# Routed experts of the second layer with the weights as the loaded operand, two blocks of rows streamed against them

## What is computed

```python
top_w, top_i = lax.top_k(softmax(xf @ gate_w.T), 6)
h = silu(einsum('ecd,edi->eci', xb, w1)) * einsum('ecd,edi->eci', xb, w3)
ob = einsum('eci,eid->ecd', h, w2)
y = zeros((T, D)).at[t_s].add(ob[buf_idx] * w_s[:, None])
```

## Time and profile before

| | |
|---|---|
| median of three runs | 1563.26 us (1562.28 to 1563.59) |
| span of the profiled execution, first to last instruction | 1559.5 us |
| what the runs lie above that span | 2.8 to 4.1 us |
| mean granted TensorE clock over the span | 0.953 |
| moved by DMA | 269.12 MB, 173 GB/s on average |

### The profile page before, as it was taken

One profiled execution on the slowest core, in us unless ns is written; L12 is line 12 of the kernel. 1 busy time (PEld: TensorE's weight loads), 2 busy tenths in 40 slices (PEclk: granted clock), 3 DMA queues, 4 the chain that ended last, 5 costly groups with the idle time before them and its releaser, 6 DMA issues.

```text
span 1559.5 us, 23674 instructions
## 1 busy us (share of the span) xinstructions
PE 1332.1 (85%) x8228; PEld 808.5 (52%) x8228; DVE 997.9 (64%) x1752; ACT 738.5 (47%) x1259; POOL 595.8 (38%) x462
## 2 busy tenths in 40 slices
PE   0047565599999599899899999999999999999997
PEld 0023252244444365566565666666666666666664
DVE  8999988979897658888545444444444444444222
ACT  4466654645554453441255454444544444454332
POOL 2343443444342343320143444344444444444343
PEclk9987866799999799999999999999999999999999
DMA  3557545678996775541278898988989998898665
GB/s 104 170 163 199 148 115 136 130 195 178 230 239 161 192 224 168 169 132 40 95 188 209 199 210 200 206 201 201 208 192 219 194 205 207 202 208 170 116 105 75
DMA packets 224178, 269.12 MB, mean 173 GB/s; under 512 B 148608, under 2 KB 148736, under 8 KB 223936
## 3 DMA queue, kind: packets, MB, share of 16 engines
q1 hardware_dynamic: 187408, 175.58, 42.5%
q0 software_dynamic: 36656, 92.03, 29.6%
HBM read 167.87 MB, written 70.32 MB: 153 GB/s over the span
## 4 chain that ended last, share of the span: by engine, by line
PE 67%; DVE 21%; issue 5%; ACT 3%; DMA 2%; POOL 0%; SPq 0%; POOLq 0%; DVEq 0%; ACTq 0%
PE psG L1832 38%; PE psO L1881 20%; DVE wkFD L1371 5%; PE psH L1849 3%; DVE wkFD L1353 2%; DMA ST<-W 2%; PE psX L1793 2%; DVE wkFN L1346 2%; DVE wkFD L1342 2%; DVE Wlo L1632 2%; DVE wkFN L1378 1%; DVE wkFN L1356 1%; DVE wkFD L1363 1%; PE psX L1731 1%; DVE H L1651 1%
## 5 line engine op out<-in xcount | busy, mean ns | idle before, releaser
L1832 PE MATMUL psG<-Whi,XSp 128*128 128x352 f16 (+2 forms) x3000 | 671.4, 329 | 11.4 <-issue 9.8
L1832 PEld LDWEIGHTS psG<-Whi,XSp 128*128 128x128 f16 x3000 | 295.3, 100 | 211.7 <-issue 37.5
L1881 PE MATMUL psO<-Whi,HS 128*128 128x512 f16 (+1 forms) x1180 | 390.5, 383 | 0.5 <-DVE OB L1671 0.5
L1832 PE MATMUL psG<-Wlo,XSp 128*128 128x352 f16 (+2 forms) x1500 | 389.0, 329 | 0.0
L1072 POOL DMA_INDIRECT out<-OB,posb x128 | 202.7, 1584 | 416.4 <-ACT OB L1279 412.7
L1632 DVE SCALAR_TENSOR_TENSOR Wlo<-ST,Whi 128x1088 f16<-128x1088 f32 (+1 forms) x116 | 149.6, 1291 | 212.0 <-ACT Whi L1225 204.1
L1651 DVE SCALAR_TENSOR_TENSOR H<-H,psG 128x352 f32<-128x352 f32 (+1 forms) x215 | 105.3, 490 | 242.5 <-ACT H L1244 226.8
L1881 PE MATMUL psO<-Wlo,HS 128*128 128x512 f16 (+1 forms) x590 | 226.3, 384 | 0.0
L1244 ACT ACTIVATE H<-psG 128x352 f32<-128x352 f32 (+1 forms) x215 | 95.3, 443 | 235.0 <-PE psG L1832 226.9
L1832 PEld LDWEIGHTS psG<-Wlo,XSp 128*128 128x128 f16 x1500 | 149.2, 99 | 93.4 <-issue 7.8
L1881 PEld LDWEIGHTS psO<-Whi,HS 128*128 128x128 f16 x1180 | 117.2, 99 | 118.2 <-issue 5.4
(11 more groups left out here) (219 smaller groups left out, 1550.3 us busy)
## 6 DMA issues: line engine op xcount, KB each, us to landing
ST<-W SPq DMA_DIRECT2D x130, 544.0 KB
ST<-W SPq DMA_DIRECT2D x23, 512.0 KB
slots<-OB SPq DMA_DIRECT2D x39, 256.0 KB
wkK<-fT SPq DMA_DIRECT2D x32, 256.0 KB
xrows<-XG SPq DMA_DIRECT2D x20, 256.0 KB, 3.4
y0rows<-x SPq DMA_DIRECT2D x8, 512.0 KB, 5.3
y0rows<-OB POOLq DMA_DIRECT2D x16, 256.0 KB, 4.7
out<-OB SPq DMA_DIRECT2D x16, 256.0 KB
```

Of the source, the lines that this page charges most:

```text
L1832: op = M.matmul(o, hx[:, x, q * P:q * P + P], w(half_, off + c, nn), start=first, stop=last)
L1881: op = M.matmul(psO[bank(o)][:, :], hs(n)[:, x, q * P:q * P + P], columns[n](half_, off0 + q * 512, 512), start=(q == 0 and x == 0 and hal ...
```

## The change

In the routed part of the second layer two blocks make a pair, 64 pairs in all. Gate and up load a 128-column piece of the weights and stream 2 x 128 rows of x against it, from two neighbouring slots of `XSp`, which now lie in one buffer. The result has the inner columns on the partitions, as `down` wants them, so H is not turned. A pair has three tiles t = 3p + c: the first 128 gate columns with the first 128 of up, the second 128 of both, and the last 96 of gate with the last 32 of up, then 64 columns of up. For these 64 the high and the low part stand side by side as one loaded piece of 128 columns; streamed are x high and x low, so that all four products are made in 8 matmuls and the two halves of the partitions are added afterwards. The tiles use five PSUM banks in turn. ACT takes a tanh of each tile, DVE the products, ACT the high part and DVE the low part of H. The packed weights of the 32 experts are laid out anew (each piece has 1024 columns and 64 of the last 256; in SBUF with the low parts 1152), the one-hot buffers move into the gaps, x has four gather buffers instead of three, and the loop's order is written anew. Numbers and sizes of DMAs stay as they are. The core of the diff:

```diff
+def ring(z):
+    return z % 4 if z < 71 else (z - 71) % 4
+def ring_before(z):
+    return max(y for y in range(z) if ring(y) == ring(z))
+def place1(e):
+    return e % SLOTS1 * 4608 if e < 32 else 18432 + (e - 32) * 4352
+def spread(u):
+    return u // 1024 * 1152 + u % 1024
...
     for m, e in enumerate([32, 33] + list(range(32))):
         for c in range(4):
             pool = 2 <= m < SLOTS1
-            out.append((1, e, c * 1088, 1088, (m + 4) % SLOTS1 * 4352 + c * 1088, "pool" if pool else "dve"))
+            out.append((1, e, c * 1088, 1088, place1(e) + c * (1152 if e < 32 else 1088), "pool" if pool else "dve"))
     return out
...
-    yield "weight", R1
-    for j in range(NB1 + 2):
-        n = R1 + j
-        yield from ahead(n)
-        if n < NBLK:
-            yield "gu_pe", n
-            yield "gu", n
-        if 0 <= j - 1 < NB1:
-            yield "h_turn", n - 1
-        if 0 <= j - 2 < NB1:
+    def turn(n, pe):
+        if n < NBLK and by_pe(xslot(n)) == pe:
+            yield ("turn" if pe else "x_turn"), xslot(n)
+    def pair_weights(p):
+        if p >= 2:
+            ready = 63 + 4 * ((2 * p - 6) // 4) if p >= 3 else 59
+            yield from weights(2 if p < 6 else 1, min(ready, len(PIECES)))
+    def tile_in(t, what):
+        if 0 <= t < 3 * PAIRS:
+            yield what, t
+    yield "gather", R1 + 3
+    for n in (R1, R1 + 1):
+        yield from turn(n, True)
+        yield "weight", n
+    yield "clear", 0
+    for p in range(PAIRS + 1):
+        n = R1 + 2 * p
+        for m in (n + 4, n + 5):
+            if m < NBLK:
+                yield "gather", m
+        yield from turn(n + 2, False)
+        yield from tile_in(3 * p, "f_gu")
+        yield from tile_in(3 * p - 1, "f_split")
+        yield from pair_weights(p)
+        yield from tile_in(3 * p + 1, "f_gu")
+        if p < PAIRS:
+            yield "f_split", 3 * p
+        yield from turn(n + 2, True)
+        yield from tile_in(3 * p + 2, "f_gu")
+        yield from turn(n + 3, True)
+        if p < PAIRS:
+            yield "f_split", 3 * p + 1
+        if p >= 1:
             yield "down", n - 2
-        if j >= 3:
-            ready = 63 + 4 * ((j - 5) // 4) if j >= 5 else 59
-            yield from weights(2 if j < 12 else 1, min(ready, len(PIECES)))
+        yield from pair_weights(p)
+        if p >= 1:
+            yield "down", n - 1
+        for m in (n + 2, n + 3):
+            if m < NBLK:
+                yield "weight", m
     yield "end", 0
...
         A0 = RT[0][:, :, :].rearrange("p q c -> p (q c)").bitcast(F16).rearrange("p (n c) -> p n c", n=32)
         B0 = RT[1][:, 0:2, :].rearrange("p q c -> p (q c)").bitcast(F16)[:, 0:32 * NB0].rearrange("p (n j) -> p n j", n=32)
-        AB = [[W[:, at:at + 512].rearrange("p (r n) -> p r n", r=4) for W, at in pair]
-              for pair in (((Whi, 26112), (Whi, 26624)), ((Wlo, 26112), (Wlo, 26624)), ((Whi, 27136), (Wlo, 27136)))]
+        gaps = [Wlo[:, e * 4608:e * 4608 + 4608].rearrange("p (r n) -> p r n", r=4)[:, :, 1024:1152] for e in range(4)]
+        AB = [gaps[0:2], gaps[2:4], [W[:, 27136:27648].rearrange("p (r n) -> p r n", r=4) for W in (Whi, Wlo)]]
         idt = OT[:, 0:128]
+        XG1 = [XG[i][:, :] for i in range(3)] + [OH[:, 0:D + 32]]
+        FH = [RT[0][:, :, :].rearrange("p q c -> p (q c)")[:, i * 768:i * 768 + 768].rearrange("p (t c) -> p t c", t=3)
+              for i in range(2)]
+        FU = [RT[0][:, 3, i * 256:i * 256 + 256] for i in range(2)]
+        FS = [RT[1][:, :, :].rearrange("p q c -> p (q c)").bitcast(F16)[:, i * 1536:i * 1536 + 1536].rearrange(
+            "p (x t c) -> p x t c", x=2, t=3) for i in range(2)]
         idx = [sb("idx0", [P, 39], U32), posb[:, :].bitcast(U32)]
...
                 eng.wait_ge(b_gu, S1 + 2 * (z - S1) + 2)
             else:
-                eng.wait_ge(b_gu, R1 + z - 71 + 1)
+                eng.wait_ge(b_fgu, 3 * ((z - 71) // 2) + 3)
         def rows_stored(f):
...
+        def f_psum(t):
+            return (psG[0][0], psG[0][1], psG[1][0], psG[1][1], psH)[t % 5]
         l_bank = [psG[1][1], psX]
...
+                        x_there(eng, 70)
+                        x_read(eng, xslot(S1 - 3 + j))
+                    if j >= 4:
+                        x_read(eng, xslot(n - 4))
+                        eng.wait_ge(b_wsl, j - 3)
+                    to, there = XG1[j % 4], d_g1[j % 4]
                 G.indirect_dma_start(
-                    out=XG[g % 3][:, 0:w], out_offset=None, in_=X[l][:, :],
-                    in_offset=bass.IndirectOffsetOnAxis(ap=idx[l][:, j:j + 1], axis=0)).then_inc(d_g[g % 3], 16)
+                    out=to, out_offset=None, in_=X[l][:, :],
+                    in_offset=bass.IndirectOffsetOnAxis(ap=idx[l][:, j:j + 1], axis=0)).then_inc(there, 16)
             def down(n):
                 what, l, j = kind(n)
...
                     A.copy(hs(n)[:, 0, 0:w], bank_[:, 0:w]).then_inc(b_hshi, 1)
+            def f_gu(t):
+                p, c = divmod(t, 3)
+                rows = 96 if c == 2 else P
+                eng.wait_ge(b_fgu, t + 1)
+                if t == 0:
+                    eng.wait_ge(b_clear, 1)
+                if p >= 2:
+                    eng.wait_ge(b_flo, t - 5)
+                if c == 2:
+                    if p >= 2:
+                        eng.wait_ge(b_fh, t - 5)
+                    A.copy(FU[p % 2][0:64, :], f_psum(t)[64:128, 256:512]).then_inc(b_flow, 1)
+                A.activation(FH[p % 2][0:rows, c, :], f_psum(t)[0:rows, 0:256], ACT.Tanh,
+                             scale=0.5 * UN).then_inc(b_ftanh, 1)
+            def f_split(t):
+                p, c = divmod(t, 3)
+                eng.wait_ge(b_fh, t + 1)
+                if p >= 2:
+                    eng.wait_ge(b_down, R1 + 2 * p - 2)
+                A.copy(FS[p % 2][:, 0, c, :], FH[p % 2][:, c, :]).then_inc(b_fhi, 1)
             def h_low(n):
...
             def weight(n):
                 j = n - R1
-                g, e = NB0 + j, j // 4
-                eng.wait_ge(d_g[g % 3], 16 * (g // 3 + 1))
+                e = j // 4
+                gathered(eng, 71 + j)
                 if j >= 8:
-                    eng.wait_ge(b_outa, g - 7)
-                V.tensor_copy(WSL[:, n % 8:n % 8 + 1], XG[g % 3][:, D + e:D + e + 1]).then_inc(b_wsl, 1)
+                    eng.wait_ge(b_outa, NB0 + j - 7)
+                V.tensor_copy(WSL[:, n % 8:n % 8 + 1], XG1[j % 4][:, D + e:D + e + 1]).then_inc(b_wsl, 1)
+            def clear(_):
+                for i in range(2):
+                    op = V.memset(FH[i][:, 2, :], 0.0)
+                op.then_inc(b_clear, 1)
+            def f_gu(t):
+                p, c = divmod(t, 3)
+                rows = 96 if c == 2 else P
+                H, ps, gain = FH[p % 2][:, c, :], f_psum(t), 0.5 * XS * UN * UN
+                eng.wait_ge(b_ftanh, t + 1)
+                V.scalar_tensor_tensor(out=H[0:rows, :], in0=H[0:rows, :], scalar=1.0, in1=ps[0:rows, 0:256],
+                                       op0=ALU.add, op1=ALU.mult).then_inc(b_fsil, 1)
+                if c < 2:
+                    eng.wait_ge(b_fsil, t + 1)
+                    V.scalar_tensor_tensor(out=H, in0=H, scalar=gain, in1=ps[:, 256:512], op0=ALU.mult,
+                                           op1=ALU.mult).then_inc(b_fh, 1)
+                    return
+                U = FU[p % 2][0:64, :]
+                eng.wait_ge(b_flow, p + 1)
+                after(V.tensor_tensor(U, U, ps[0:64, 256:512], ALU.add))
+                eng.wait_ge(b_fsil, t + 1)
+                V.scalar_tensor_tensor(out=H[64:96, :], in0=H[64:96, :], scalar=gain, in1=ps[96:128, 0:256],
+                                       op0=ALU.mult, op1=ALU.mult)
+                V.scalar_tensor_tensor(out=H[0:64, :], in0=H[0:64, :], scalar=gain, in1=U, op0=ALU.mult,
+                                       op1=ALU.mult).then_inc(b_fh, 1)
+            def f_split(t):
+                p, c = divmod(t, 3)
+                eng.wait_ge(b_fhi, t + 1)
+                V.tensor_tensor(FS[p % 2][:, 1, c, :], FH[p % 2][:, c, :], FS[p % 2][:, 0, c, :],
+                                ALU.subtract).then_inc(b_flo, 1)
             def gu(n):
                 l, a = kind(n)[1], n % 2
...
+            def f_gu(t):
+                p, c = divmod(t, 3)
+                n = R1 + 2 * p
+                ps, s, at = f_psum(t), ring(xslot(n)), place1(p // 2)
+                if c == 0:
+                    for h in range(2):
+                        x_there(eng, xslot(n + h))
+                    for k in last_pieces(n):
+                        eng.wait_ge(*low(k))
+                if t == 0:
+                    eng.wait_ge(b_h, R1)
+                if t == 4:
+                    eng.wait_ge(b_hslo, R1)
+                if t >= 5:
+                    eng.wait_ge(b_fh, t - 4)
+                def x(which, q):
+                    return XSall[:, s:s + 2, which, q * P:q * P + P]
+                def sums(cols):
```

(76 more changed lines are left out.)

77 lines of the change are left out of this document (35 added, 42 removed).

## The result

The changed kernel takes 1626.53 us (median of 4 runs, 1617.93 to 1633.98) against 1563.42 us before: 1.0397 times as long, 95% interval 1.0351 to 1.0443. The forecast was 1546.6 us and faster, in a range of 1539 to 1560. The measured time lies 80 us above the forecast, on the other side of the kernel before.

A forecast was written before the change was run, and what follows sets the result against it. The prediction took PE, full in the last loop, as the bound. Span 1559.5 - 23.7 (PE work saved) + 7.0 (stalls at the ends) = 1542.8 us, with 3.8 from span to measured time 1546.6 us; range 1539 to 1560.

The forecast's parts named there:

- the order in a pair: Last loop: copies, splits, loads, transposes, gathers and scatters all arrive before PE needs them; costed at nothing.
- rival 3: ACT's in-order queue: late first pieces of 24 later experts hold tanh and copy of x, 0.35 us each; 1555 us, chance 0.09.
- The matmul of 256 columns: Gate and up on PE: 109.2 ns start to start, 68 a pair, 0.27 us more per pair than before.
- rival 2: Gate and up: two streamed pieces each pay a start, 112.6 ns a matmul; 1561.4 us, no difference; chance 0.07.
- rival 5: Gate and up: weight loads show, 151 ns a matmul, 1729 us; chance 0.03.
- The pair of 11.78 us: PE's work per pair in the last loop, 0.37 us less than before; 23.7 us saved over 64 pairs.
- the stall before pair 1: Loop start: no down ahead of pair 1, so PE waits for ACT's copy, tanh and copy of x; +1.75 us.
- the last split: Loop end: ACT's split of the last tile stands behind evictions of two downs, so down starts 1.9 us late.
- Rival 4: Last loop: DMA engines, at share 0.94, are the bound; a pair stays at 12.15 us, total 1570 us; chance 0.08.
- the sum for pieces 51 to 66: Pairs 2 to 5, four weight pieces each: stalls of 3.6, 2.9 and 0.2 us in pairs 3, 4, 5; 6.7 us.
- rival 1: First pairs flow: stalls from early pieces and the last split shrink to the old loop's; 1539 to 1541 us, chance 0.15.
- Rival 6: Pair loop runs half serial, a previous pair's buffer not free, each tile waiting for DVE; chance 0.01 where costing more than gained.

The follow-up runs named there:

- experiment 2: Changed kernel with a pair's two gathers and two weight-column copies ahead of the two downs, so before the scatters: 1547.35 us.
- experiment 1: Changed kernel with the first load of a new expert's four pieces ahead of the DMA transpose of x: 1582.9 us.
- experiment 5: Changed kernel with the two gathers between the two downs, behind the first scatter and ahead of the second: 1629.05 us.
- Experiment 8: Changed kernel with weight pieces spread two a pair from pair 1 on, gathers still behind the scatters: 1558.07 us.
- experiment 7: As experiment 5, but the next even block's DMA transpose is yielded in the pair before, ahead of the second weight piece: 1549.9 us.
- Experiment 3: Changed kernel with PE turning every block of the last loop, so no DMA transposes there: 1574.16 us.
- experiment 9: Changed kernel with gathers ahead of the scatters and weight pieces spread two a pair from pair 1 on: 1536.49 us.
- experiment 6: Control: changed kernel with only DVE's two routing-weight copies moved ahead of the downs, gathers still behind the scatters: 1634.24 us.

## Why the prediction was wrong

**What failed** is the paragraph on the order in a pair, which ended in "All this I cost at nothing". It cost 79 us, the difference between the changed kernel and experiment 2. Three things in it fell.

- *"its load stands behind the DMA transpose, which is free from tile 2 of the pair before on, 4 us before this pair."* I took the buffer's release as the transpose's only condition. It also waits for its gather, which stands on POOL behind two scatters, which wait for two evictions at the pair's end. The place of a moved step in each queue had to be followed through POOL as well as SP.
- *"Pieces land in 3.8 to 6.2 us, scatters in 4.9; ... only a landing of over 10 us would reach PE."* The rows were from the kernel before, where one scatter and one gather go out every 6 us (at 1202.12 and 1204.00, then at 1207.97 and 1209.86). With two gathers, two scatters, a transpose and a load within a few microseconds, gathers landed in 8.5 us (median), a piece behind a transpose in 9.7, and in experiments 1 and 5 a transpose behind a load in 11.8 to 13.4.
- *The margins were each taken from PE's own timetable.* Each of them held for one pair, and the steps close a ring. A ring has one length, the sum of all its links, and this one was 29.8 us where two pairs have 23.5. That ACT's queue then holds up everything behind a piece is rival 3. It was the right mechanism with a wrong size: 0.35 us for each of 24 experts, 8.4 in all. Experiment 8, where ACT no longer waits, gives 68 us back, some of them in the first pairs. But experiment 5 loses 82 us against experiment 2 without such waits, so rival 3 is one of two rings and not the whole.

**What held.** The matmul of 256 columns: 109.2 ns forecast and found (24 in 2.62 us), so rivals 2 and 5 fall. The Trainium skill's 81 ns for a load and a matmul of 128 columns ("TensorE: Matmul & The Clock Gate", Back-to-back issue gap) is not seen here either: the turn's eight matmuls of 128 columns, a load with each, take 0.45 us, 56 ns each. The prediction gave 120 ns at 256 columns as what follows from that figure, without a working, and it does not follow. The same section has 131 ns at 512 columns, and a straight line between the two gives 98 ns, an estimate below the 109 found. So the page did not speak for a slower kernel, and its 131 ns are not seen either: 18 matmuls of 512 columns take 3.88 us, 216 ns each. The pair of 11.78 us, found at 11.75 in experiment 2. ACT at 7.2 and DVE at 7.7 of 11.8 us a pair: in experiment 2 they are busy for 330 and 345 of 600 us, which is 6.5 and 6.8. The first tile, forecast for 768.5 and found at 768.04, and the stall before pair 1, forecast as 1.75 us and found as 1.36 (the changed kernel's timeline of PE):

```profile
768.04 0.38 PE L1988 MATMUL psG<-XSp,Whi 128*128 128x256 f16 x2 [1.15 <-ACT XSp L1300]
...
777.88 0.38 PE L1988 MATMUL psG<-XSp,Whi 128*128 128x256 f16 x2 [1.36 <-ACT XSp L1300]
```

The copy of x waited for in pairs 3 and 4, forecast as 3.6 and 2.9 us, found as 3.15 and 3.01:

```profile
813.46 0.61 PE L1917 MATMUL psX<-ident,XG 128*128 128x128 f16 x8 [3.15 <-ACT XSp L1300]
...
830.51 0.61 PE L1917 MATMUL psX<-ident,OH 128*128 128x128 f16 x8 [3.01 <-ACT XSp L1300]
```

And the last split, forecast at 1.9 us, found as 1.53:

```profile
1619.77 0.39 PE L2059 MATMUL psO<-Whi,RT 128*128 128x512 f16 x1 [1.53 <-DVE RT L1766]
```

Rival 4, full DMA engines, is refuted by experiments 2 and 7: the same transfers in another order, at 199 and 198 GB/s, and PE full. (Experiment 3 has fewer transfers and can't decide it.) The total forecast, 1546.6 us, is what the change gives once the ring is cut (1547.35). That does not save the prediction: it was made for the order in the diff. That the two numbers differ by less than 1 us is in part luck: experiment 2's stalls in the first pairs are some 2 us above their term, and 64 pairs of 11.75 us are 2 us below theirs.

**On the sum for pieces 51 to 66**: 6.7 us forecast. The changed kernel's two waits are 6.2 us. Between experiments 2 and 9 PE's idle time in the first 100 us falls by 9.1 us when the pieces are spread, a third more than the term. Either way rival 1, that the first pairs flow, falls. Rival 6, a tile that waits for DVE, is not seen: PE waits for DVE once in the stretch, 0.8 us.

**What stays open.** Which part of a landing of 10 us and more is the crowd and which the order within one DMA queue was not measured by itself, so that transfers take longer because they come in a crowd is argued here and not shown. Nor was it tried how many gathers ahead would do without moving them.

## What to carry to other kernels

When a loop is reordered, write down for each queue what stands ahead of every transfer, and follow the conditions round until they return to the same step; then add up the links with landings from a kernel that issues its transfers as closely as the new one will (7 to 13 us in these rings, where the rows before had 4 to 6), and compare the sum with the time of the turns it serves. Margins one by one do not show such a ring. Issue what has a long way to go (gathers) ahead of what only ends something (scatters), and keep a step that waits for a freed buffer from standing ahead of one that is already free to go.

## What the runs showed of the hardware that was not expected

- The DMA engines' share of busy time is a bad measure of how full they are. The changed kernel had 0.91 at 182 GB/s, experiment 2 0.87 at 199, experiment 8 0.98 at 196.
- DMA transposes cost more of that share than they move. Without them (experiment 3) it is 0.67 at 172 GB/s, with them (experiment 2) 0.87 at 199; per GB/s that is 0.0039 against 0.0044, for one block of 128 rows out of two.
- A kernel held by such a ring varies from run to run: 1618 to 1634 us for the changed kernel, 1613 to 1636 for experiment 5, against 1547.0 to 1548.6 for experiment 2. All five kernels in which PE waits for transfers time after time (the changed one, experiments 1, 5, 6 and 8) spread by 1.0 to 1.4%, all others by 0.1 to 0.6%. A wide spread is itself a hint that arrivals, and no engine, set the beat.
- After some waits of about 2 us and more PE ran 3 to 6 us of its next tiles at the lower clock level: after 6 of 37 in the changed kernel, after 14 of 22 in experiment 5, with the same matmuls. The clock's mean in the steady stretch was 0.98 in the first and 0.95 in the second. That is how two kernels lose the same time with 65 and 52 us of waits.
